# A graph kernel's relational sums in two steps: 128x32 masks for four chunks at a time, then seven quads per tile

## The chip, the cores and the metric

One core of one Trainium2 chip. The metric is the device time in microseconds (us), the median of three runs. Everything is float32. The profile comes from one execution of the same program.

## The reference, cut to what matters

The graph has 6250 nodes of 256 features and 106250 edges sorted by destination, one of them per node a self-loop; each edge has one of eight types. Three relational layers are followed by one attention layer:

```python
for l in range(3):
    xr = jnp.einsum('nd,rde->rne', x, W_rel[l])          # eight tables, one per edge type
    agg = jax.ops.segment_sum(xr[edge_type, src], dst, num_segments=N)
    x = jax.nn.relu(agg + x @ W_root[l] + bias[l])
# then h = x @ Wv + bv, scores q[src] + k[dst], softmax by dst, and the weighted sum of h[src]
```

A layer norm and a ReLU stand before the first layer and before the attention layer, and each of the two has a residual.

## The kernel before, in words

**Data.** Nodes are cut into 49 tiles of 128 (`NT`). A layer's eight transformed tables lie in DRAM, 1 MB per node tile. The edges without the self-loops are packed into 787 chunks of 128 (`CH`), in the order of their destination. Four chunks are a quad (called a group in the code), so there are 197 (`GROUPS`). Self-loops don't go through the chunks: VectorE adds them from PSUM when a table is made, and for the first layer from reloaded tables (`add_first_loops`, L814, eight multiply-adds per tile, whose running sum stands in PSUM).

**Gathers.** POOL runs `gather_pass` (L585) once per layer, four times in all: 787 indirect DMAs (L592), each fetching 128 rows of 1 KB into one slot of a ring of 40 (`RINGS` is 10 quads). Quad n may be issued when `released` has reached n - 9. That semaphore is counted by SP in `relay` (L716), a loop over the quads: it waits until quad n has landed, counts `in_order` (L721), then for quad m = n - 8 (`LAG`) it waits until every tile that reads quad m has gone far enough (`added`), and counts `released` (L732). SP's relay thus ties the release of one quad to the landing of the eighth after it. A pass can begin when all tables of the layer are stored (`wait_tables`).

**Relational sums.** Tile i reads 18 chunks (`SLOTS`) from a first chunk that is computed on the chip. ScalarE builds for each a 128x128 mask of edge against node (`build_mask`, L1344: 18 Abs, L1357, and five Relu, L1364). TensorE multiplies mask by ring slot 18 times into `sum_ps` (`sum_tile`, L1619, L1632), the 256-wide rows found through registers. A chunk is read by every tile that it touches. In the first layer the root product (L1625, two matmuls) opens the sum.

**The rest of a tile in the layers 0 and 1.** VectorE adds the loops' part and writes z (`sum_up`, L1042), TensorE transposes z (`turn`, L1531), ScalarE applies the ReLU (L1255), TensorE makes the next layer's table of the tile (`transform`, L1546: five banks, ten matmuls), ScalarE copies banks 0 to 2 to `stage` (L1264) and VectorE bank 3 (L785), VectorE adds the self-loops (L810) and the root part (L795), and ScalarE's queue stores 1 MB. The program order on TensorE puts the transform of tile i - 1 between the second and the third quad of tile i (L1656 to L1668). In layer 2 the transform is replaced by the product with Wv (`to_h`, L1678), after a layer norm on VectorE (L1067), and `store_h` writes 130 KB.

**Before the layers** the first table is made, 7.09 us per tile (the transform, L1546, back to back), and beside it DVE, POOL, ACT and PE plan the edges at fixed tiles (`before_layers_at`, L394). POOL ends its planning at L582. **The attention pass** (L1764 on) has its own chain of transposes, exponentials and sums (L1758), and the same `relay`.

The float32 matmul appears in the trace as two LDWEIGHTS records (PEld) and two MATMUL records (PE).

## Time and profile before

| what | value |
|---|---|
| median of three runs | 5282.95 us (5263.98 to 5283.96) |
| span of the profiled execution | 5218.2 us |
| time of the profiled execution outside its span | not recorded; the median stands 64.8 us above the span |
| PE / ACT / DVE / POOL busy | 3531.3 / 2203.5 / 1648.4 / 3049.7 us |
| before the layers | 0 to 369 us |
| layer 0 / layer 1 / layer 2, first gather to last | 369 to 1538 / 1588 to 2743 / 2786 to 3915 us |
| attention, first gather to last | 3950 to 5182 us |
| mean granted TensorE clock | 0.82 of 2.4 GHz |

Busy time counts an engine's own instructions. Register, branch and semaphore instructions aren't in it, so an engine can be "idle, issue" while its sequencer works on the next instruction. A releaser that reads "remote" or "issue" wasn't found by the profile.

### The profile page before, as it was taken

The page shows a single profiled execution, that of the slowest core. Times are in us where ns is not written, and L with a number is a line of the kernel's source. Part 1 is how long each engine was busy: PE and PEld are TensorE (multiplying, and loading weights), DVE is VectorE, ACT ScalarE, POOL GpSimd, SP SyncE. Part 2 cuts the span into 40 slices and gives each one's busy share as a digit, 9 for nine tenths or more (in the row PEclk, how much of TensorE's full clock was granted, in tenths as well). Part 3 has the DMA queues.
Part 4 walks back from the last instruction along what each step waited for, and adds up shares of the span by engine and source line. Part 5 has one row for each costly group of instructions (what it writes and reads, how often), then busy time and mean ns, then how long its engine had stood idle before and what let it go on. Part 6 is the DMA issues. An engine that isn't in the chain of part 4 may idle for free.

```text
span 5218.2 us, 55702 instructions
## 1 busy us (share of the span) xinstructions
PE 3531.3 (68%) x12674; PEld 2474.9 (47%) x12674; DVE 1648.4 (32%) x4423; ACT 2203.5 (42%) x6033; POOL 3049.7 (58%) x3295
## 2 busy tenths in 40 slices
PE   9986877788785777677775544545454666566666
PEld 4444554555553445445453333334333555455555
DVE  4533333334341222222221111111113444444444
ACT  2332443344432434343343333333334555555555
POOL 1135666666655666666664666666664566556664
PEclk9997988898887888888887777767677878878788
DMA  6554555555543444344443333333332333333332
GB/s 212 193 199 130 184 186 176 178 186 192 183 169 126 132 133 139 125 136 138 131 137 95 103 103 103 103 101 105 102 102 77 93 98 96 95 95 97 98 96 75
DMA packets 240046, 681.43 MB, mean 131 GB/s; under 512 B 60188, under 2 KB 111988, under 8 KB 215028
## 3 DMA queue, kind: packets, MB, share of 16 engines
q0 software_dynamic: 152400, 419.03, 27.6%
q10 hardware_dynamic: 57240, 186.43, 9.7%
q1 hardware_dynamic: 30092, 72.34, 3.8%
q8 instruction: 128, 2.10, 0.2%
q14 instruction: 186, 1.52, 0.1%
HBM read 501.99 MB, written 175.58 MB: 130 GB/s over the span
## 4 chain that ended last, share of the span: by engine, by line
PE 31%; another core or an unknown queue 28%; ACT 14%; issue 14%; DVE 9%; DVEq 2%; ACTq 1%; DMA 0%; SPq 0%; POOL 0%
PE bank L1546 13%; PE sum_ps L1632 9%; ACT masks L1357 4%; ACT masks L1451 4%; PE sum_ps L1758 3%; DVE root L810 3%; PE bank L1708 2%; DVEq L809 2%; ACT wide L1428 2%; PE bank L1714 2%; ACT masks L1364 1%; PE turn_ps L1531 1%; ACT stage L1467 1%; ACT wide L1461 1%
## 5 line engine op out<-in xcount | busy, mean ns | idle before, releaser
L592 POOL DMA_INDIRECT ring<-table,code x2361 | 2233.3, 946 | 1357.2 <-issue 661.9
L1632 PE MATMUL sum_ps<-ring,masks 128*128 x5292 | 1403.2, 423 | 199.2 <-issue 196.9
L1632 PEld LDWEIGHTS sum_ps<-ring,masks 128*128 128x128 f32 x5292 | 1126.6, 216 | 453.9 <-issue 271.2
L1546 PE MATMUL bank<-wide,xT 128*128 128x512 f32 (+1 forms) x2744 | 1125.2, 564 | 7.9 <-issue 6.3
L592 POOL DMA_INDIRECT ring<-h_table,code x787 | 746.6, 949 | 519.3 <-SPq L732 275.0
L1357 ACT ACTIVATE masks<-node_row,local 128x128 f32<-128x128 f32 x2646 | 788.5, 388 | 27.8 <-issue 13.7
L1546 PEld LDWEIGHTS bank<-wide,xT 128*128 128x128 f32 x2744 | 515.6, 190 | 563.6 <-issue 552.0
L1255 ACT ACTIVATE xT<-turn_ps 128x256 f32<-128x256 f32 x196 | 75.5, 385 | 1429.0 <-remote 587.4
L1758 PE MATMUL sum_ps<-ring,stage 128*128 x1764 | 492.7, 426 | 76.8 <-ACT stage L1467 48.7
L1264 ACT COPY stage<-bank 128x512 f32<-128x512 f32 x441 | 243.9, 582 | 590.0 <-remote 353.6
L810 DVE SCALAR_TENSOR_TENSOR root<-bank,loops,root 128x256 f32<-128x256 f32 x686 | 331.0, 483 | 369.5 <-ACT stage L1264 179.5
L1758 PEld LDWEIGHTS sum_ps<-ring,stage 128*128 128x128 f32 x1764 | 363.2, 218 | 143.4 <-issue 94.1
L1682 PE MATMUL bank<-wide,xT 128*128 128x256 f32 x196 | 94.5, 632 | 483.6 <-ACT xT L1255 475.0
L1714 PE MATMUL bank<-ident,wide 128*128 128x128 f32 x931 | 188.5, 337 | 333.0 <-ACT wide L1461 325.7
L1531 PE MATMUL turn_ps<-ident,z 128*128 128x128 f32 x392 | 99.7, 344 | 454.5 <-DVE z L1042 313.8
L1364 ACT ACTIVATE masks<-masks 128x512 f32<-128x512 f32 (+1 forms) x735 | 366.6, 573 | 85.6 <-remote 68.9
L1428 ACT ACTIVATE wide<-bank,low_key 128x512 f32<-128x512 f32 (+1 forms) x245 | 162.8, 665 | 502.5 <-remote 284.4
L810 DVE SCALAR_TENSOR_TENSOR root<-bank,loops,bias_row 128x256 f32<-128x256 f32 x98 | 47.4, 484 | 931.1 <-ACT stage L1264 560.2
L1070 DVE TENSOR_TENSOR stage<-sum_ps,root 128x256 f32<-128x256 f32 x49 | 20.8, 425 | 915.0 <-remote 834.5
L1714 PEld LDWEIGHTS bank<-ident,wide 128*128 128x128 f32 x931 | 142.2, 177 | 351.5 <-issue 351.2
L1531 PEld LDWEIGHTS turn_ps<-ident,z 128*128 128x128 f32 x392 | 53.3, 165 | 537.4 <-DVE z L1042 351.6
L1116 DVE SCALAR_TENSOR_TENSOR wide<-bank,key,wide 128x512 f32<-128x512 f32 (+1 forms) x245 | 177.1, 723 | 406.7 <-ACT wide L1428 309.0
(216 smaller groups left out, 2504.3 us busy)
## 6 DMA issues: line engine op xcount, KB each, us to landing
table<-stage ACTq DMA_DIRECT2D x96, 1024.0 KB
back<-table ACTq DMA_DIRECT2D x49, 1024.0 KB
table<-stage SPq DMA_DIRECT2D x48, 1024.0 KB
ring<-table,code POOLq DMA_INDIRECT x2361
ring<-h_table,code POOLq DMA_INDIRECT x787
h_table<-stage ACTq DMA_DIRECT2D x49, 130.0 KB
back<-h_table ACTq DMA_DIRECT2D x49, 130.0 KB
features<-xT SPq DMA_DIRECT2D x49, 128.0 KB, 4.0
```

The lines of the kernel that those rows point to most:

```text
L592: pool.indirect_dma_start(slot(c % RING, width), None, table, bass.IndirectOffsetOnAxis(ap=code[:, c:c + 1], axis=0)).then_inc(landed[n % ...
L810: nc.vector.scalar_tensor_tensor(root[:, i, :], bank[t // 2][:, t % 2 * D:(t % 2 + 1) * D], loop_weight(i, t), root[:, i, :] if t else bia ...
L1264: nc.scalar.copy(stage[:, b, 512 * q:512 * (q + 1)], bank[q][:, :]).then_inc(evacuated[q], 1)
L1357: instruction = nc.scalar.activation(masks[:, b, s, :], node_row[:, :], ACT.Abs, scale=-1.0, bias=local[:, bass.ds(i, 1), s])
L1364: instruction = nc.scalar.activation(part, part, ACT.Relu, scale=-1.0, bias=1.0)
L1428: return nc.scalar.activation(part, score_ps[c % 2][:, 0:part.shape[1]], ACT.Identity, scale=SLOPE, bias=low_key[:, bass.ds(i, 1)])
L1451: last = nc.scalar.activation(masks[:, b, s, :], node_row[:, :], ACT.Abs, scale=-1.0, bias=local[:, bass.ds(i, 1), s])
L1531: last = nc.tensor.transpose(turn_ps[:, k, :], z[:, b, k * P:(k + 1) * P], ident[:, :])
L1546: last = nc.tensor.matmul(bank[q][:, 0:width], xT[:, b, k, :], weights[:, k, 512 * q:512 * q + width], start=(k == 0), stop=(k == K - 1))
L1632: last = nc.tensor.matmul(sum_ps[b][:, 0:D], masks[:, b, s, :], at_offset(slots[s]), start=(s == 0 and l > 0), stop=(s == SLOTS - 1))
L1714: last = nc.tensor.transpose(attn_ps[c % 2][:, s % GROUP * P:(s % GROUP + 1) * P], scores[b][:, s * P:(s + 1) * P], ident[:, :])
L1758: last = nc.tensor.matmul(sum_ps[b][:, 0:D], attn_slot(s), at_offset(where[0][s]) if s < SLOTS else own_rows[:, b, 0:D], start=(s == 0), s ...
```

## The change

Chunk sums come first, tile sums second. For each quad, TensorE multiplies four 128x32 masks (edge against the chunk's own 32 nodes, counted from its least destination) by the four ring slots, each into 32 of the 128 PSUM partitions (`sum_windows`). ScalarE copies two quads' sums at a time to SBUF (`keep_pairs`). A tile is then the sum of seven quads, with seven 128x128 masks that name the node of each of the quad's 128 rows (`sum_tile`). Each chunk is read once, and quad n of the ring is issued when the chunk sums of quad n - 10 are done (`quad_done`), with no relay in between; SP's relay stays for the attention pass. VectorE builds both kinds of masks, two instructions per tile, and ScalarE builds none. On TensorE the transform of tile i - 1 stands in one piece behind the new pairs of quads of tile i and before its seven products. SP issues the loads and stores of the layers in place of ScalarE. The running sum of `add_first_loops` moves from PSUM to SBUF. Before the layers there are new planning steps for the masks: on DVE `relative`, `spread_quads` (nine small ones), `keep_relative` and `name_rows`, on PE seven transposes and one matmul, on POOL a few more of 343 elements. The attention pass is the same but for the names of its PSUM tiles. Most tiles bring two new pairs of quads (16 chunks).

```diff
-    PARTED = 1
+    WINDOW = P // GROUP
+    SPAN = 7
+    PAIR = 2
+    NP = -(-GROUPS // PAIR)
+    SUM_RING = 4
+    CHUNKS_AT_ONCE = 2 * PAIR * GROUP
+    MASK_BATCHES = -(-CH // CHUNKS_AT_ONCE)
...
+    def first_quad(t):
+        middle = CH * (P * t + P / 2) / N
+        return max(0, min(round((middle - GROUP * SPAN / 2) / GROUP), GROUPS - SPAN))
+
+    def pairs_to(t):
+        return (first_quad(t) + SPAN - 1) // PAIR + 1 if t >= 0 else 0
...
+    def new_pairs(t):
+        pairs = range(pairs_to(t - 1), pairs_to(t))
+        half = (len(pairs) + 1) // 2
+        return pairs[:half], pairs[half:]
...
-        sum_ps = [ctx.enter_context(nc.psum_tensor(f"sum_ps{b}", [P, 512], F32)) for b in range(2)]
-        turn_ps = ctx.enter_context(nc.psum_tensor("turn_ps", [P, K, P], F32))
+        pair_ps = [ctx.enter_context(nc.psum_tensor(f"pair_ps{b}", [P, 512], F32)) for b in range(2)]
+        both_sums = ctx.enter_context(nc.psum_tensor("both_sums", [P, 512], F32))
+        sum_ps = [both_sums[:, b * D:(b + 1) * D] for b in range(2)]
+        turn_root = ctx.enter_context(nc.psum_tensor("turn_root", [P, 512], F32))
...
+        def window_masks(k):
+            return flat(masks[:, k % 2, SPAN:SPAN + CHUNKS_AT_ONCE * WINDOW // P, :]
+                        ).rearrange("p (c w) -> p c w", w=WINDOW)
...
+        def quad_sums(q):
+            return pair_sums(q // PAIR)[:, q % PAIR * D:(q % PAIR + 1) * D]
...
+            step(pool.tensor_tensor(astray, per_chunk(chunk_id), per_tile(window_start), ALU.subtract))
+            step(pool.tensor_scalar(outside, astray, 0.0, None, ALU.is_lt))
+            step(pool.tensor_scalar(astray, astray, float(GROUP * SPAN - 1), None, ALU.is_gt))
+            step(pool.tensor_tensor(astray, astray, outside, ALU.add))
...
             def gather_pass(l, table, width):
                 if l:
-                    pool.wait_ge(in_order, l * GROUPS)
+                    pool.wait_ge(quad_done, l * GROUPS)
                 for n in range(GROUPS):
-                    if n >= RINGS:
-                        pool.wait_ge(released, l * RELEASES + n - RINGS + 1)
+                    if n >= RINGS and l < L:
+                        pool.wait_ge(quad_done, l * GROUPS + n - RINGS + 1)
+                    elif n >= RINGS:
+                        pool.wait_ge(released, n - RINGS + 1)
...
-            def relay(l):
+            def relay():
...
-                    sp.wait_ge(landed[n % RINGS], 16 * gathers_to(l, n))
+                    sp.wait_ge(landed[n % RINGS], 16 * gathers_to(L, n))
...
+            def load_features(i, b):
+                if i > 1:
+                    sp.wait_ge(added, tile_added(0, i - 2))
+                sp.dma_start(first_T[:, b, :, :].rearrange("p k n -> p (k n)"), features[i * P:(i + 1) * P, :]
+                             ).then_inc(features_loaded[b], 16)
+
+            def load_back(i, b):
+                if i > 1:
+                    sp.wait_ge(back_step, loops_done(i - 2, R))
+                sp.dma_start(back[:, b, :], tables_by_node[0][i * P:(i + 1) * P, :]).then_inc(back_loaded[b], 16)
+
...
+            def store_next(l, i, b):
+                for q in range(R // 2):
+                    sp.wait_ge(evacuated[q], CREDIT + NT * l + i + 1)
+                sp.dma_start(tables_by_node[l][i * P:(i + 1) * P, :], stage[:, b, :]).then_inc(stored[b], 16)
...
+                for i in range(NT):
+                    j, b = divmod(i, 2)
+                    if l == 0:
+                        load_features(i, b)
+                        load_back(i, b)
+                    if l == L - 1:
+                        load_x(i, b)
+                        if i > 1:
+                            store_h(i - 2, j - 1, b)
+                    elif i > 1:
+                        store_next(l + 1, i - 2, b)
...
-                    nc.vector.scalar_tensor_tensor(root[:, i, :] if t == R - 1 else loop_ps, back[:, b, t * D:(t + 1) * D],
-                                                   loop_weight(i, t), loop_ps if t else root[:, i, :], ALU.mult, ALU.add
-                                                   ).then_inc(back_step, 1)
-                settle(dve, loops_done(i, R))
+                    nc.vector.scalar_tensor_tensor(root[:, i, :], back[:, b, t * D:(t + 1) * D], loop_weight(i, t),
...
+            def mask_windows(l, first, end):
+                for k in range(first, end):
+                    chunks = range(CHUNKS_AT_ONCE * k, min(CHUNKS_AT_ONCE * (k + 1), CH))
+                    if l or k > 1:
+                        reused = l * GROUPS + (2 * PAIR * (k - 1) if k > 1 else 0)
+                        dve.wait_ge(quad_done, reused)
+                    shape = [P, len(chunks), WINDOW]
+                    nc.vector.tensor_tensor(window_masks(k)[:, 0:len(chunks), :],
+                                            rel_T[:, chunks[0]:chunks[-1] + 1].unsqueeze(2).to_broadcast(shape),
+                                            node_row[:, 0:WINDOW].unsqueeze(1).to_broadcast(shape), ALU.is_equal
+                                            ).then_inc(window_masked, 1)
+
+            def mask_tile(l, i):
+                if l or i > 1:
+                    dve.wait_ge(added, tile_added(l, i - 2) if i > 1 else tile_added(l - 1, NT - 1))
+                shape = [P, SPAN, P]
+                nc.vector.scalar_tensor_tensor(masks[:, i % 2, 0:SPAN, :],
+                                               row_node[:, first_quad(i):first_quad(i) + SPAN].unsqueeze(2).to_broadcast(shape),
+                                               -float(P * i), node_row[:, :].unsqueeze(1).to_broadcast(shape),
+                                               ALU.add, ALU.is_equal).then_inc(tile_masked, 1)
+
+            def upcoming_masks(l, i):
+                if i < NT:
+                    mask_tile(l, i)
+                    mask_windows(l, batches_to(i - 1), batches_to(i))
+
...
+            def relative():
...
+                shape = [P, KM, P]
+                nc.vector.tensor_tensor(rel_n.rearrange("p (m e) -> p m e", e=P), dst_n.rearrange("p (m e) -> p m e", e=P),
+                                        least.unsqueeze(2).to_broadcast(shape), ALU.subtract).then_inc(row_step, 1)
...
+            def name_rows():
+                dve.wait_ge(row_step, ROWS_PLACED)
+                dve.wait_ge(shift_known, 1)
+                nc.vector.tensor_scalar(row_node[:, :], pair_ps[0][:, 0:KM * WINDOW], row_place[:, 0:1], far_shift[:, 0:1],
+                                        ALU.add, ALU.add).then_inc(row_step, 1)
...
+                for i in range(NT):
                     j, b = divmod(i, 2)
...
+                    sum_up(l, i, j, b)
+                    upcoming_masks(l, i + 2)
+                    if l == 0 and i + 1 < NT:
+                        add_first_loops(i + 1, (i + 1) // 2, 1 - b)
+                    next_table(l, i, j, b)
...
-            def build_mask(l, i, j, b, last=False):
...
-                for s in range(SLOTS):
-                    instruction = nc.scalar.activation(masks[:, b, s, :], node_row[:, :], ACT.Abs, scale=-1.0,
-                                                       bias=local[:, bass.ds(i, 1), s])
...
-                for c in range(PIECES):
-                    part = masks[:, b, gathered(c)[0]:gathered(c)[-1] + 1, :]
-                    instruction = nc.scalar.activation(part, part, ACT.Relu, scale=-1.0, bias=1.0)
-                instruction.then_inc(mask_ready[b], 1)
...
+            def keep_pairs(l, pairs):
+                for p in pairs:
+                    act.wait_ge(quad_done, l * GROUPS + min(PAIR * (p + 1), GROUPS))
+                    if l or p >= SUM_RING:
+                        act.wait_ge(added, tile_added(l, tiles_of_pair(p - SUM_RING) - 1) if p >= SUM_RING
+                                    else tile_added(l, -1))
+                    width = D * (min(PAIR * (p + 1), GROUPS) - PAIR * p)
+                    nc.scalar.copy(pair_sums(p)[:, 0:width], pair_ps[p % 2][:, 0:width]).then_inc(pair_kept, 1)
...
+                for i in range(NT + 1):
+                    early, late = new_pairs(i) if i < NT else ((), ())
+                    keep_pairs(l, early)
+                    if i:
+                        j, b = divmod(i - 1, 2)
+                        use = (l + 1) * USES[b] + j
+                        relu_turned(use, b, transformed[b], NB * use)
+                    keep_pairs(l, late)
+                    if i:
+                        for q in range(R // 2 - 1):
+                            keep_bank(l + 1, use, b, q)
...
+            def turn_relative():
+                pe.wait_ge(row_step, ROWS_SPREAD)
+                pe.wait_ge(broken_copied, 1)
+                turn_edges(rel_n, row_step)
...
+            def sum_windows(l, pairs):
+                for p in pairs:
+                    if l or p > 1:
+                        pe.wait_ge(pair_kept, l * NP + p - 1 if p > 1 else l * NP)
+                    for q in range(PAIR * p, min(PAIR * (p + 1), GROUPS)):
+                        k = GROUP * q // CHUNKS_AT_ONCE
+                        pe.wait_ge(window_masked, l * MASK_BATCHES + k + 1)
+                        pe.wait_ge(landed[q % RINGS], 16 * gathers_to(l, q))
+                        for c in chunks_of(q):
+                            at_row = c % GROUP * WINDOW
+                            last = nc.tensor.matmul(pair_ps[p % 2][at_row:at_row + WINDOW, q % PAIR * D:(q % PAIR + 1) * D],
+                                                    window_masks(k)[:, c % CHUNKS_AT_ONCE, :], slot(c % RING, D),
+                                                    start=True, stop=True)
+                        last.then_inc(quad_done, 1)
+
+            def sum_tile(l, i, j, b):
+                pe.wait_ge(tile_masked, l * NT + i + 1)
+                pe.wait_ge(pair_kept, l * NP + pairs_to(i))
+                if l == 0:
+                    pe.wait_ge(features_loaded[b], 16 * (j + 1))
                     for k in range(K):
                         nc.tensor.matmul(sum_ps[b][:, 0:D], first_T[:, b, k, :], first_root[:, k, :],
                                          start=(k == 0), stop=False)
-                for c in pieces:
-                    settle(pe, l * GROUPS + groups[c])
-                    pe.wait_ge(mask_ready[b], use + 1)
-                    pe.wait_ge(in_order, l * GROUPS + groups[c])
-                    for s in gathered(c):
-                        last = nc.tensor.matmul(sum_ps[b][:, 0:D], masks[:, b, s, :], at_offset(slots[s]),
-                                                start=(s == 0 and l > 0), stop=(s == SLOTS - 1))
-                    if c in PART_ENDS:
-                        last.then_inc(added, 1)
...
+                for i in range(NT + 1):
+                    early, late = new_pairs(i) if i < NT else ((), ())
+                    sum_windows(l, early)
+                    if i:
+                        j, b = divmod(i - 1, 2)
+                        turn_sum(l, j, b)
+                    sum_windows(l, late)
+                    if i:
+                        transform((l + 1) * NT + i - 1, (l + 1) * USES[b] + j, b, AHEAD + REST)
+                    if i < NT:
+                        sum_tile(l, i, i // 2, i % 2)
```

## Rows read from the trace of the kernel before

**Rows 1.** The page's first line: the span.
```profile
span 5218.2 us, 55702 instructions
```
**Rows 2.** Busy time by stretch, all engines; the columns are in its first line.
```profile
core 0: us, PE busy (x) PEld busy (x) DVE busy (x) ACT busy (x) POOL busy (x), PEclk, DMA share, GB/s
...
369.00:1538.00 1169.00, 900.69 (x3007) 617.17 (x3008) 444.35 (x998) 467.95 (x1292) 743.65 (x786) 0.86 0.54 181
...
1588.00:2743.00 1155.00, 829.10 (x2713) 552.95 (x2714) 239.34 (x507) 463.85 (x1287) 742.84 (x786) 0.84 0.42 134
...
2786.00:3915.00 1129.00, 562.40 (x1968) 427.27 (x1968) 166.04 (x640) 408.68 (x1197) 743.46 (x786) 0.71 0.35 103
```
**Rows 3.** Groups of instructions, the gathers: busy us, mean ns | idle before them.
```profile
L592 POOL DMA_INDIRECT ring<-table,code x2361 | 2233.3, 946 | 1357.2 <-issue 661.9 <-SPq L732 560.0 <-DMA table<-stage 135.4
...
L592 POOL DMA_INDIRECT ring<-h_table,code x787 | 746.6, 949 | 519.3 <-SPq L732 275.0 <-issue 244.3
```
**Rows 4.** Timeline of POOL: first and last gather of each pass (start us, us).
```profile
369.55 1.11 POOL L592 DMA_INDIRECT ring<-table,code  x1 [43.42 <-DMA table<-stage]
...
1538.44 0.95 POOL L592 DMA_INDIRECT ring<-table,code  x1 [0.30 <-issue]
1588.72 0.94 POOL L592 DMA_INDIRECT ring<-table,code  x1 [49.34 <-DMA table<-stage]
...
2743.29 0.94 POOL L592 DMA_INDIRECT ring<-table,code  x1 [0.30 <-issue]
2786.85 0.94 POOL L592 DMA_INDIRECT ring<-table,code  x1 [42.62 <-DMA table<-stage]
...
3915.69 0.95 POOL L592 DMA_INDIRECT ring<-table,code  x1 [0.30 <-issue]
3950.09 0.94 POOL L592 DMA_INDIRECT ring<-h_table,code  x1 [33.46 <-issue]
```
**Rows 5.** Timeline of one tile's wait in layer 2, POOL and DVE.
```profile
3026.65 0.95 POOL L592 DMA_INDIRECT ring<-table,code  x1 [0.30 <-issue]
3027.90 0.95 POOL L592 DMA_INDIRECT ring<-table,code  x1 [0.30 <-issue]
...
3031.94 0.94 POOL L592 DMA_INDIRECT ring<-table,code  x1 [3.10 <-SPq L732]
...
3032.21 0.42 DVE L1074 SCALAR_TENSOR_TENSOR root<-stage 128x256 f32<-128x256 f32 x1
...
3033.19 0.95 POOL L592 DMA_INDIRECT ring<-table,code  x1 [0.30 <-issue]
```
**Rows 6.** Timeline of DVE: the first masked chunk of the attention pass.
```profile
3956.84 0.95 DVE L1181 TENSOR_SCALAR masks<-masks,ring 128x128 f32<-128x128 f32 x4 [10.51 <-issue]
```
**Rows 7.** Timeline of PE: root product in layer 0, then the end of layer 1.
```profile
1554.78 1.03 PE L1625 MATMUL sum_ps<-first_root,first_T 128*128 128x256 f32 x4
...
2769.47 4.48 PE L1632 MATMUL sum_ps<-ring,masks 128*128 x20
2774.53 0.44 PE L1531 MATMUL turn_ps<-ident,z 128*128 128x128 f32 x2 [0.57 <-DVE z L1042]
2775.44 8.00 PE L1546 MATMUL bank<-wide,xT 128*128 128x512 f32 x20 [0.47 <-ACT xT L1255]
```
**Rows 8.** Groups of instructions: weight loads, masks, copies, first loops and a wide VectorE operation.
```profile
L1632 PEld LDWEIGHTS sum_ps<-ring,masks 128*128 128x128 f32 x5292 | 1126.6, 216 | 453.9 <-issue 271.2
...
L1357 ACT ACTIVATE masks<-node_row,local 128x128 f32<-128x128 f32 x2646 | 788.5, 388 | 27.8 <-issue 13.7 <-DMA table<-stage 9.2 <-DVE stage L785 2.4
...
L1264 ACT COPY stage<-bank 128x512 f32<-128x512 f32 x441 | 243.9, 582 | 590.0 <-remote 353.6 <-PE bank L1546 188.2 <-issue 47.6
...
L821 DVE SCALAR_TENSOR_TENSOR bank<-back,loops,bank 128x256 f32<-128x256 f32 x294 | 143.4, 488 | 32.8 <-issue 2.3 <-DVE bank L821 0.5
...
L944 DVE SCALAR_TENSOR_TENSOR masks<-ring,masks 128x896 f32<-128x896 f32 x1 | 1.1, 1093 | 0.0
```
**Rows 9.** Timeline of POOL: the end of its planning.
```profile
326.05 0.09 POOL L582 MEMSET credit<- 1x1 f32 x1 [1.85 <-DMA need<-need_dram]
```

346 lines of the change are left out of this document (158 added, 188 removed).

## The prediction, made before the changed kernel was seen

> **What bounds the kernel now.** I read the profile in four steps. First the busy times by stretch [rows 2]: in the three layers TensorE is busy for 77, 72 and 50% of the time, ScalarE 40, 40 and 36%, DMA 54, 42 and 35%. None is full. POOL has the same 743 us in all three, and that looks low too, but busy time leaves out its issue work. So second, the gathers in a row [rows 5]: they start 1.25 us apart (3026.65, 3027.90; 3031.94, 3033.19) though each lasts 0.95. The missing 0.30 us is "issue", and it makes most of the 661.9 us behind "issue" in the group's row [rows 3]. A pass of 787 gathers can't be shorter than 786 x 1.25 = 982.5 us. Third, what a pass takes from its first gather to its last [rows 4]: 1168.9 in layer 0, 1154.6 in layer 1, 1128.8 in layer 2. So POOL is the bound for 85% of each layer, and the rest is waits: 186.4 + 172.1 + 146.3 = 504.8 us. The group's row names them: 560.0 us behind SP's L732, the relay's "released" [rows 3] (some 0.3 us in each is issue time that is there anyway).
>
> Fourth, why it waits [rows 5]: the gather at 3027.90 ends at 3028.85, the next starts 3.1 us later, in a layer in which TensorE is half idle. The ring isn't full of unread work; the release of a quad is tied to the landing of the eighth after it, so that POOL is let go only two quads ahead of what has landed, and to a tile's second part. A landing takes about 2.0 us: the fourth gather of the attention pass ends at 3950.09 + 3 x 1.25 + 0.95 = 3954.8 [rows 4], and the first mask that reads its quad starts at 3956.84 [rows 6]. That latency is paid again and again.
>
> **The change, part by part.** My yardstick is 787 / 49 = 16.06 gathers per tile, 20.1 us.
>
> *The release.* Quad n now waits only for the chunk sums of quad n - 10. Those come one or two quads at a time, and in between TensorE does one transform and one tile's sum, 8.0 us and 3.1 us. POOL has ten quads, 50 us, in the ring, so it should never wait as long as TensorE needs less than 20.1 us per tile. All 504.8 us then go. This is nearly the whole forecast, so the next step is the one that matters.
>
> *TensorE per tile.* A 256-wide record costs 4.48 / 20 = 0.224 us, hence 0.448 us per mask product, and a transform 8.0 us, a transpose pair 0.44 [rows 7]. Before: 18 x 0.448 + 8.0 + 0.44 = 16.5 us in layer 1 (busy 829 / 49 = 16.9 [rows 2] agrees). After: 7 x 0.448 = 3.1, plus 8.0, plus 0.44, plus 16 chunk products. No row has a product with 32 columns. Its nearest row has 128 columns and the same 256-wide moving side: 0.448, as if the four column groups went one after the other; a quarter of it, 0.112, if they went side by side. I keep both ends: 7.2 or 1.8 us. Layer 1 is then 18.7 or 13.3 us, layer 0 with its root product (1.03 [rows 7]) 19.8 or 14.3, layer 2 with a product by Wv of the same size as that 11.8 or 6.4. I take the nearest row, 0.448. All lie below 20.1, in layer 0 by only 0.3. TensorE's work may thus rise and the layers still get shorter. The clock weighs against this: it was granted at 0.84 in layer 1, that is, 32% of the time at 1.2 GHz, with the engine 28% idle. With 13.3 us of work at that mean clock the engine needs 15.8 us and stays inside; with 18.7 us it is nearly never idle and I expect the clock up, but at 0.93 it would be at 20.1.
> The Trainium skill (TensorEngine Tiling (Array Packing), "Key Properties") says that different tiles load weights and multiply in parallel, but that a change of the tiling mode drains the engine, which this change does four times a tile. No row here shows either. By the first, the work would be near 13 to 15 us and the sum the same.
>
> *ScalarE.* It loses the masks, 18 x 0.388 us (788.5 in all) and the Relus behind them, and gets two copies of pairs per tile at 0.58 [rows 8]. Neither ended a wait above: nothing gained but slack, and 1.2 us of new copies that lie under the transform. They cost nothing while the transform covers them; without it 1.2 us a tile.
>
> *VectorE.* It gets a mask of 896 elements, 1.09 us by the only operation of that size, and one of 512, some 0.65 by the same row's scale [rows 8]. With the table's ten operations (some 6 us) and, in layer 0, eight first loops at 0.49 (3.9 us) it has about 12 us of 20.1. The window masks wait for chunk sums that come behind the transpose on TensorE, so VectorE holds back the loops and the table's evacuation until the transform starts, and ends them some 10 us later, before the tile's sum (12 us). Cost 0; cover 2 us in layer 0.
>
> *SP.* Loads and stores of a layer move behind waits on one in-order queue: a store of tile i - 2 stands before the loads for tile i + 1. Each is wanted a whole tile (20 us) later; cost 0. In the relay's place nothing waits on SP in the layers.
>
> *POOL's pace beside VectorE.* The new masks read two SBUF operands, and so do the first loops now. The nearest row: L1074, with two SBUF operands, lies wholly inside the gather of 3031.94, which took 0.94 us and was followed after 0.30 [rows 5]. I take 3 us per pass for odd delays, +9 us (0 to 20).
>
> *Between two passes.* E is the end of the last gather. Quad 195 has landed at E - 1.75; its chunk sums are done near E. Then in order: transform 46 (8.0), sum of tile 47 (3.1), three chunks (1.3), transpose (from it to the transform's start 0.91 [rows 7]), transform 47 (8.0), sum of tile 48 (3.1), 0.6 for VectorE's z, 0.91 and, from the last transform's start to the next pass, 2786.85 - 2775.44 = 11.4 [rows 4, 7]. Sum 37.3, and 1.0 more in layer 0, against 42.6 and 49.3: -5.3 and -11.0. In layer 2 the last tile has 11 products fewer behind the last landing, 11 x 0.448: -5. Together -21 (0 to -35).
>
> *Before the layers.* DVE gets one subtraction of 896 elements (1.09 [rows 8]) and some fifteen smaller ones, PE seven transposes. TensorE sets the pace there, and DVE has 4 to 5 us free per tile, so part is hidden: +8 (0 to +16, all of them at 1.09). POOL's extra planning (some 5 us) ends against a slack of 369.55 - 326.05 = 43.5 us [rows 4, 9]: 0. The attention pass isn't touched: 0.
>
> **The sum.** -504.8 + 9 - 21 + 8 = -509 us. On the profiled execution 5218.2 [rows 1] - 509 = 4709. Its own time around the span isn't recorded; the median stands 64.8 us above it and I carry that over: 5282.95 - 509 = **4774 us**.
>
> **Rivals.**
> 1. *TensorE becomes the bound in the layers 0 and 1.* The chunk products cost 0.448, and drains or stretches at 1.2 GHz take another tenth: 18.7 / 0.9 = 20.8 and 19.8 / 0.9 = 22.0 us per tile, (0.7 + 1.9) x 49 = 127 us: **4901** (4820 to 5000). For it: the margin of 0.3 us, and the transform in one piece, which bunches the work. Against: products with a quarter of the columns should take less than the full ones.
> 2. *VectorE's masks hold up POOL.* Each new microsecond with two SBUF operands delays the gathers by as much: (8 x 0.42 + 1.7) us per tile in layer 0, 1.7 in each other layer, (5.1 + 1.7 + 1.7) x 49 = 417 us: **5191**. Against it stands the gather around L1074 [rows 5]. The Trainium skill (SBUF — State Buffer, "SBUF: two separate sides") has this as its rule: the two engines share a port pair, and a VectorE instruction with two SBUF inputs locks out a GpSimd one that reads SBUF. The trace's gather of 0.94 us doesn't show it.
> 3. *Slower: the small products can't hide their weight loads.* Place: between a quad's eight record pairs. A load takes 0.216 us [rows 8] and lies beside the matmuls today. Laid bare it adds 0.43 us per chunk, 6.9 us per tile: 25.6 us in layer 1, 26.7 in layer 0, (5.5 + 6.6) x 49 = 593 us: **5367**. It decides from the point at which the two excesses eat 509 us, that is 10.4 us in all: (10.4 + 1.7) / 32 = 0.38 us bare per chunk. Against it: a load of 32 columns should be shorter than one of 128, and loads overlap in every burst of the trace. The Trainium skill (TensorE: Matmul & The Clock Gate, "Part 3: Packing small matmuls") says that a load passes matmuls in flight only when its row group differs, which it doesn't among these four. For full-size products the trace disagrees: 20 records at 0.224 us each [rows 7], with loads of 0.216 beside them.
> 4. *The waits stay*, because something else than the relay holds the ring, such as the first chunk sums being late at each pass. The change would bring the tails and cost the planning, 5283 - 21 + 8 = **5270**. Against: 10 quads are 50 us.
>
> **How the numbers follow.** Forecast 0.70; rival 1 0.19; rival 2 0.04; rival 3 0.05; rival 4 0.02, within 0.5% of before (about what a measurement of this kernel can tell from no change). The range takes the forecast's own bounds (down to 4746: no delays, nothing added ahead, longer tails saved) and rival 1 to its end at 5000; left out are the rivals 2 to 4, 0.11, and a few per cent of bad luck. Faster 0.93, same 0.02, slower 0.05.
>
> **What would show it.** Right: the first gather to the last takes 983 to 990 us in each of the three layers, starts stay 1.25 us apart, and POOL's waits for a semaphore inside a pass nearly vanish; TensorE idles for landings; the gap between passes is 35 to 40 us. The length of a quad's burst (8 records x 0.224 = 1.8 us, or a quarter) tells which price the products have. Wrong: passes 0 and 1 well over 990 us with TensorE always busy (rival 1, or 3 if the burst exceeds 3 us), gathers longer than 1 us beside masks (rival 2), or POOL waiting on `quad_done` while TensorE idles (rival 4). The forecast fails as a whole if layer 2, which has 8 us to spare, isn't near 985.

## The result: half a per cent, not ten

The changed kernel takes **5249.31 us** (median of 7, 5236.56 to 5251.97) against 5281.34 us (7 runs, 5263.16 to 5283.96) for the one before in the same job (a job is one set of runs on one chip): ratio **0.9946**, 95% interval 0.9932 to 0.9959. Two later jobs gave 0.9956 (0.9942 to 0.9970) and 0.9953 (0.9929 to 0.9977). In one more job, of which more below, both kernels took 13 to 16% less and the order turned round: 4542.19 us (4 runs, 4538.37 to 4545.96) against 4436.48 us (7 runs, 4433.76 to 4440.49), ratio **1.0238**, interval 1.0221 to 1.0256. Every run here, timed or not, was recorded by the profiler.

The work per engine fell as the change says. The page's first lines for the changed kernel:

```profile
span 5249.8 us, 48781 instructions
## 1 busy us (share of the span) xinstructions
PE 3232.7 (62%) x14171; PEld 1974.0 (38%) x14171; DVE 1905.0 (36%) x4736; ACT 1240.1 (24%) x2949; POOL 3146.9 (60%) x3305
```

ScalarE lost 963 us, TensorE 299 us, and VectorE, which builds the masks now, gained 257 us. But the passes are as long as they were. Busy time by stretch, the four passes in order, answering [rows 2] (each stretch runs from the pass's first gather to its last):

```profile
core 0: us, PE busy (x) PEld busy (x) DVE busy (x) ACT busy (x) POOL busy (x), PEclk, DMA share, GB/s
375.90:1542.40 1166.50, 777.98 (x3418) 430.21 (x3419) 513.44 (x1066) 150.23 (x274) 775.63 (x786) 0.80 0.54 178
1599.30:2739.30 1140.00, 718.59 (x3130) 372.20 (x3131) 313.58 (x588) 150.94 (x274) 762.54 (x786) 0.77 0.42 134
2793.50:3925.90 1132.40, 451.94 (x2434) 275.59 (x2434) 238.69 (x717) 82.47 (x184) 779.67 (x787) 0.63 0.36 102
3965.10:5211.00 1245.90, 773.40 (x3591) 637.63 (x3591) 571.25 (x1676) 698.80 (x1859) 749.07 (x786) 0.78 0.35 95
```

Passes of 1166.5, 1140.0 and 1132.4 us stand against 1168.9, 1154.6 and 1128.8 [rows 4], and POOL's time above 1.25 us per gather is 184, 158 and 150 us against 186, 172 and 146: 491 us in the layers where the prediction had 504.8 going to nothing. The gathers' groups, answering [rows 3]:

```profile
L674 POOL DMA_INDIRECT ring<-table,code x2361 | 2320.8, 983 | 1273.7 <-issue 733.1 <-remote 378.7 <-DMA table<-stage 96.7
L674 POOL DMA_INDIRECT ring<-h_table,code x787 | 750.0, 953 | 535.1 <-SPq L814 285.8 <-issue 249.3
```

SP has gone from the layers' row. In its place stands "remote", a releaser that the profile didn't find. It is `quad_done`, the only semaphore POOL still waits for there. One tile of layer 1, in the timelines of POOL, DVE and PE:

```profile
2008.22 0.95 POOL L674 DMA_INDIRECT ring<-table,code  x1 [0.30 <-issue]
...
2013.23 0.95 POOL L674 DMA_INDIRECT ring<-table,code  x1 [0.30 <-issue]
2017.38 0.95 POOL L674 DMA_INDIRECT ring<-table,code  x1 [3.20 <-remote]
...
2006.05 0.42 DVE L924 TENSOR_TENSOR root<-turn_root,root 128x256 f32<-128x256 f32 x1
2017.05 0.42 DVE L1233 TENSOR_TENSOR z<-both_sums,root 128x256 f32<-128x256 f32 x1 [10.58 <-remote]
...
2004.91 3.19 PE L1767 MATMUL both_sums<-masks 128*128 128x256 f32 x14
2008.02 1.07 PE L1753 MATMUL pair_ps<-ring,masks 128*32 128x256 f32 x16
2017.53 0.69 PE L1644 MATMUL turn_root<-ident,z 128*128 128x128 f32 x2 [8.44 <-DVE z L1233]
```

By its records TensorE ends the tile's sum at 2008.1 and two pairs of windows at 2009.1. VectorE's z, which needs nothing but that sum, starts at 2017.05, 9 us later, 2.9 us after POOL's last gather ended. In the semaphores' own records `added` goes up at 2017.03 and `quad_done`, twice, at 2017.12 and 2017.21, though the two records that count it start at 2008.28 and 2008.71. So POOL waits for a signal from TensorE, and here gets it only once POOL itself has stopped. The other tiles agree: the middle value of z's delay behind its sum is 7.4 us in layer 0 and 8.1 us in layer 1. In layer 2 only 17 of 46 are over 2 us, but POOL's 32 waits there end 8.9 us (middle value) behind the last record of the chunk sums. That is the same picture as one tile before the change [rows 5], where I had read the relay into it.

### The profile page after: what moved, and what is told of

It reads as the page before. It is cut to its first block, busy times and chain, and to the rows that moved or that the text cites. A ratio compares the mean times of both kernels' runs of the same rounds, so it can differ in the third digit from the quotient of the medians.

```text
span 5249.8 us, 48781 instructions
## 1 busy us (share of the span) xinstructions
PE 3232.7 (62%) x14171; PEld 1974.0 (38%) x14171; DVE 1905.0 (36%) x4736; ACT 1240.1 (24%) x2949; POOL 3146.9 (60%) x3305
## 4 chain that ended last, share of the span: by engine, by line
PE 36%; another core or an unknown queue 34%; issue 13%; ACT 9%; DVE 7%; DVEq 0%; ACTq 0%; POOL 0%; DMA 0%; POOLq 0%
PE bank L1659 19%; PE pair_ps L1753 5%; PE pair_ps L1864 3%; PE both_sums L1767 3%; ACT masks L1565 3%; ACT wide L1542 2%; DVE root L939 2%; PE turn_root L1644 2%; PE bank L1814 2%; PE bank L1820 1%; ACT stage L1581 1%; ACT wide L1575 1%; DVE z L1233 1%; PE bank L1796 1%
## 5 line engine op out<-in xcount | busy, mean ns | idle before, releaser
L674 POOL DMA_INDIRECT ring<-table,code x2361 | 2320.8, 983 | 1273.7 <-issue 733.1
L1659 PE MATMUL bank<-wide,xT 128*128 128x512 f32 x2352 | 1148.9, 644 | 45.0 <-ACT xT L1445 44.7
L674 POOL DMA_INDIRECT ring<-h_table,code x787 | 750.0, 953 | 535.1 <-SPq L814 285.8
L1767 PE MATMUL both_sums<-masks 128*128 128x256 f32 x2058 | 539.7, 420 | 340.5 <-ACT masks L1501 206.3
L1501 ACT COPY masks<-pair_ps 128x512 f32<-128x512 f32 x297 | 173.2, 583 | 2184.5 <-remote 1693.8
L1767 PEld LDWEIGHTS both_sums<-masks 128*128 128x128 f32 x2058 | 441.0, 216 | 431.8 <-issue 358.2
L1864 PE MATMUL pair_ps<-ring,stage 128*128 x1764 | 508.4, 437 | 136.4 <-issue 91.3
L1753 PE MATMUL pair_ps<-ring,masks 128*32 128x256 f32 x4722 | 442.8, 491 | 99.7 <-DMA ring<-table,code 76.2
L1864 PEld LDWEIGHTS pair_ps<-ring,stage 128*128 128x128 f32 x1764 | 371.1, 223 | 205.3 <-issue 154.2
L939 DVE SCALAR_TENSOR_TENSOR root<-bank,loops,root 128x256 f32<-128x256 f32 x686 | 331.1, 483 | 161.3 <-ACT stage L1507 73.2
L1565 ACT ACTIVATE masks<-node_row,local 128x128 f32<-128x128 f32 x931 | 282.1, 396 | 0.0
L1371 DVE TENSOR_SCALAR masks<-masks,ring 128x128 f32<-128x128 f32 x882 | 203.0, 298 | 213.7 <-issue 212.7
L1753 PEld LDWEIGHTS pair_ps<-ring,masks 128*32 128x32 f32 x4722 | 148.9, 129 | 295.4 <-issue 242.4
```

The costliest lines, as they stand in the source:

```text
L674: pool.indirect_dma_start(slot(c % RING, width), None, table, bass.IndirectOffsetOnAxis(ap=code[:, c:c + 1], axis=0)).then_inc(landed[n % ...
L939: nc.vector.scalar_tensor_tensor(root[:, i, :], bank[t // 2][:, t % 2 * D:(t % 2 + 1) * D], loop_weight(i, t), root[:, i, :] if t else bia ...
L1371: last = nc.vector.tensor_scalar(masks[:, b, s, :], masks[:, b, s, :], -FAR, source, ALU.mult, ALU.add)
L1565: last = nc.scalar.activation(masks[:, b, s, :], node_row[:, :], ACT.Abs, scale=-1.0, bias=local[:, bass.ds(i, 1), s])
L1659: last = nc.tensor.matmul(bank[q][:, 0:width], xT[:, b, k, :], weights[:, k, 512 * q:512 * q + width], start=(k == 0), stop=(k == K - 1))
L1753: last = nc.tensor.matmul(pair_ps[p % 2][at_row:at_row + WINDOW, q % PAIR * D:(q % PAIR + 1) * D], window_masks(k)[:, c % CHUNKS_AT_ONCE, ...
```

## The experiments

Two words for what follows: a record is one of the two MATMUL entries that a product leaves in the trace, and a pause is a stretch in which POOL issues no gather. The theories I took in turn: A, TensorE's last signals come out only when more products follow; B (B1), gathers without a pause hold TensorE up; B2, the rows' data do; B3, a budget of instructions; C, the records are early and TensorE has more work than they show; L, a fixed price per pause; R, a rate.

**e1: more products.** 24 products of 128x256 before a tile's turn in layers 0 and 1.

```
+    ...                                       # waits until bank[0] is free
+    for _ in range(24):
+        nc.tensor.matmul(bank[0][:, 0:D], ident[:, :], weights[:, 0, 0:D], start=True, stop=True)
     turn_sum(l, j, b)
```

> 24 extra products of 128x256 into an idle bank stand on TensorE between a tile's early windows and its turn in layers 0 and 1 (about 2.6 us per tile, in an idle stretch of some 8 us). The changed kernel's trace shows TensorE's signal of a tile's sum 6.5 to 9 us after the sum's last product, about 2.7 us after GpSimd's last gather of a run. Theory A (TensorE's last signals come out only when more products follow): VectorE's z starts within 1 us of the sum's end, GpSimd's waits in layers 0 and 1 (340 us) mostly go, time 4900 to 5000 us. Theory B (the signals are held up while GpSimd issues gathers back to back, whatever TensorE does): z still 6 to 9 us late, waits and time unchanged, 5235 to 5265 us. Theory C (the products' records are early, and TensorE really computes until the signal comes): the extra products come on top, about 2.6 us per tile, 5249 + 98 x 2.6 = 5500 us.

5466.64 us. I had counted a product as one record of 0.11 us; it is two of 0.22, so the edit added 10.6 us per tile and made TensorE the bound: tiles of 24.8 and 24.3 us in layers 0 and 1, TensorE busy throughout. z mostly came 0.04 to 0.9 us after its sum, but with POOL stopped. Nothing was told apart. (5466.64 us lies near what theory C had, but by the added 10.6 us per tile, not by C's reason.)

**e2: a quarter of the gathers** in layers 1 and 2.

```
-    for c in chunks_of(n):
+    for c in (chunks_of(n) if l in (0, L) else chunks_of(n)[:1]):
```

> In layers 1 and 2 only one chunk in four is gathered (the other slots of the ring keep old rows), so GpSimd has 5 us of gathers per tile in place of 20. It shows what the other four engines need by themselves. If the tile's own chain of products, copies and masks takes 23 us, as long as the pass of now (theory C): layers 1 and 2 stay at 1130 to 1140 us each. If the signals are held up by back-to-back gathers (theory B): GpSimd is quiet nearly always, z follows the sum within 0.5 us, and the two passes fall to what the engines need, 13 to 19 us per tile, 640 to 930 us each. Theory A (more products must follow): z stays 2 to 9 us late in the quiet kernel too, passes over 950 us.

4064.2 us. POOL's timeline in layer 1:

```profile
1749.62 1.40 POOL L674 DMA_INDIRECT ring<-table,code  x1 [8.16 <-PE pair_ps L1753]
1751.32 0.94 POOL L674 DMA_INDIRECT ring<-table,code  x1 [0.30 <-PE pair_ps L1753]
...
1762.93 1.41 POOL L674 DMA_INDIRECT ring<-table,code  x1 [8.16 <-PE pair_ps L1753]
```

A tile takes 13.31 us, z follows its sum by 0.04 us, the passes take 616 and 462 us. Layer 0 of the same run, with all its gathers, has z 7.45 us behind its sum (middle value of 45 tiles). The chain of a tile is short when POOL is quiet: C falls as a matter of work, and so does A.

**e3: by itself.** TensorE and VectorE signal back and forth, with and without gathers.

> A kernel of its own that computes nothing of the reference: TensorE does two products of 128x256 and signals, VectorE copies the sum out and signals back, in rounds; in phases without gathers, beside 80 gathers of GpSimd without a pause (100 us), the same with 24, with 4 further products and with 16 small ones (128x32) behind each signal, with ScalarE in TensorE's place, and beside 48 plain loads of SP. Theory B: beside gathers a round with TensorE takes many us (the signals come out only as the gathers stop), with ScalarE and beside plain loads 1 to 1.5 us. Theory A: rounds beside gathers are long with nothing behind the signal and short with 24 products behind it. Theory C, or anything that belongs to the kernel and not to the chip: every round takes 1 to 1.6 us (3.5 to 4 us with 24 products behind), with or without gathers.

Windows of the run, the first without gathers, the next two in the first phase with them, then the one with 24 further products and the one with ScalarE asking:

```profile
core 0: us, PE busy (x) PEld busy (x) DVE busy (x) ACT busy (x) POOL busy (x), PEclk, DMA share, GB/s
5.00:30.00 25.00, 20.16 (x40) 11.23 (x38) 3.97 (x10) 0.00 (x0) 0.00 (x0) 1.00 0.00 0
35.00:58.00 23.00, 18.36 (x37) 10.55 (x36) 3.81 (x9) 0.00 (x0) 17.52 (x19) 1.00 0.36 108
66.00:122.00 56.00, 10.37 (x20) 5.88 (x20) 2.12 (x5) 0.00 (x0) 42.39 (x45) 1.00 0.35 105
225.00:280.00 55.00, 11.72 (x20) 5.94 (x21) 0.42 (x1) 0.00 (x0) 41.59 (x45) 0.51 0.35 105
555.00:582.00 27.00, 4.53 (x21) 3.64 (x20) 11.72 (x33) 13.13 (x33) 20.60 (x22) 0.66 0.35 106
```

Nine rounds beside the gathers take 2.59 us as in quiet. Then TensorE does 20 product records in 56 us, **2.80 us each**, at a granted clock of 1.00 as at 0.51, until 8 to 12 us behind the last gather. With ScalarE in its place a round takes 0.76 to 0.98 us beside the same gathers; beside 48 plain loads of SP (235 GB/s) TensorE's take 1.65 us, and the same behind the loads (shorter than the 2.59 us of the first phase, for which I have no reason). B holds, and the kernel isn't needed for it.

**e4: what about the gathers does it.**

> A kernel of its own again: rounds of two products of 128x256, a signal and 24 further products (52 product records, 11.2 us without gathers), beside 80 gathers. In the ping-pong run before, TensorE did some 40 to 50 product records at full speed beside back-to-back gathers and then one per 2.80 us until some 10 us after the last gather. Eight phases, each with one thing changed: as it was; the 24 products with 64 columns; gathered rows of 64 columns (256 bytes); a small memset of GpSimd behind each gather (about 0.3 us); a wait for landing after every 8 gathers; bf16 operands in the 24 products; a wait for landing after every 4 gathers; 240 memsets in place of the gathers. Theory B1 (GpSimd's unbroken issuing of gathers blocks TensorE's instructions, whatever they read): 2.8 us per record also with 64 columns, with narrow rows and with bf16; the memsets alone do nothing; a wait after every 8 gathers brings TensorE back to 11.2 to 14 us per round. Theory B2 (the rows' data in SBUF are in the way of what TensorE reads): with 64 columns or with narrow rows the cost per record falls to a quarter, 0.7 us, or goes. Theory B3 (a budget of instructions that only long quiet gives back): the waits after 8 or 4 gathers change nothing, rounds stay over 50 us.

One window from each of the first seven phases, in the order of the text above:

```profile
core 0: us, PE busy (x) PEld busy (x) DVE busy (x) POOL busy (x), PEclk, DMA share, GB/s
20.00:100.00 80.00, 21.01 (x46) 11.02 (x44) 0.42 (x1) 60.51 (x65) 0.54 0.35 105
220.00:300.00 80.00, 9.44 (x31) 8.54 (x30) 0.00 (x0) 53.77 (x57) 0.50 0.32 95
445.00:525.00 80.00, 17.91 (x30) 8.73 (x31) 0.42 (x1) 58.41 (x62) 0.50 0.12 26
635.00:715.00 80.00, 80.00 (x372) 70.42 (x372) 2.97 (x7) 64.98 (x103) 1.00 0.28 84
755.00:835.00 80.00, 80.00 (x373) 70.42 (x372) 2.97 (x7) 47.44 (x51) 1.00 0.28 83
890.00:960.00 70.00, 9.46 (x28) 3.63 (x28) 0.00 (x0) 52.94 (x57) 0.52 0.35 105
1010.00:1090.00 80.00, 80.00 (x372) 70.44 (x371) 2.97 (x7) 40.83 (x44) 1.00 0.24 72
```

After the fast start (which is in the first window), some 30 records in 80 us whether they have 256 or 64 columns, float32 or bf16 operands, and whether the gathers move 105 or 26 GB/s: B2 falls. With 0.30 us more between gathers, or a wait for landing after 8 or 4, TensorE does 372: B1 holds, B3 falls. In the eighth phase, 240 memsets in place of the gathers, it does 520 in 116 us, at full speed too.

**e5, e6, e7: room between the gathers.** GpSimd writes a spare tile behind each quad (128x256) or each gather (128x1); e7 does the like by itself.

```
+    def space():
+        pool.wait_ge(prep_step, steps[0])
+        steps[0] += 1
+        pool.memset(spare[:, :], 0.0).then_inc(prep_step, 1)
...
+    if (c + 1) % 4 == 0:
+        space()
```

> The changed kernel with one memset of 128x256 (0.30 us) by GpSimd behind each quad of gathers, in all four passes: 0.08 us more per gather, 1.2 us per tile of 16 gathers. Theory B1 (unbroken issuing of gathers at 1.25 us starves TensorE's instructions, 2.80 us each, and the ring then fills): the pause per quad is enough, or nearly, TensorE's signals come within 1 us, GpSimd's waits of 3 us per tile go, a pass of the layers takes about 197 x (5.0 + 0.3) = 1045 us in place of 1132 to 1166, and the time is 4900 to 4980 us (below that if the attention's pass gains too). Rival (GpSimd waits for TensorE because the tile's chain of products, copies and masks takes 23 us whatever the gathers do): the memsets only fill waits, passes stay at 1130 to 1170 us, time 5240 to 5260 us. Rival (a pause per quad is too seldom): waits stay and 236 us come on top, up to 5485 us.

> The same with a memset of 128x1 (about 0.06 us and its own start) behind each single gather. Theory B1 with the distance between two gathers as what counts: a step of 1.31 to 1.45 us per gather, passes of 1030 to 1140 us without any wait, time 4850 to 5250 us by that step. If the short memset hides in the gather's own gap (the step stays at 1.25 us) and any other instruction between two gathers is enough to let TensorE go on, passes come down to 985 us and the time to 4750 us. Rival (the chain takes 23 us per tile): unchanged, 5240 to 5260 us.

> The ping-pong kernel with 80 gathers per phase and rounds of 52 product records (11.2 us alone). GpSimd's memset between gathers: 128x1 behind each, 128x256 behind every 4th, 128x1 behind every 4th, 128x64 behind every 4th, 128x256 behind every 8th, 128x64 behind every 2nd, and no memset but a wait that is already met behind each. In the run before, 0.30 us behind each gather gave 11.2 us in every round, nothing between them 2.80 us per product record. Theory B1 (what counts is how dense the gathers are): there is a mean step between 1.25 and 1.55 us from which the rounds are clean; the 0.30 us behind every 4th (1.33 us mean) are near it, the short ones behind every 4th and the wait alone stay bad. Rival (what counts is that GpSimd executes another instruction at all): all of them are clean, the wait alone perhaps too.

4666.23 and 4540.18 us, passes of 1050 to 1024 and 1014 to 998 us, and the passes look like a hit for B1 until one sees the kernel before beside them: **4431.09 us**. In e7 nothing was slow, not even with no memset at all. So this job was in another condition, and the three runs say nothing on spacing, but much on the condition. What differs is written in the trace: of the 3148 x 16 = 50,368 updates that the gathers' landings make, the traces of e5 and e6 hold 50,179 and 50,048, those of before and after 11,263 and 12,723. I call the two kinds "free" (over 99% of the updates kept, TensorE not held up) and "held" below. In the three free traces with the kernel z follows its sum by 0.04 us in the middle, beside gathers mostly 1.25 us apart.

**e8, e9, e10: once more.** The job was of the held kind again, on the same chip number as the free one.

> The changed kernel once more, in three rounds, because the kernel before took 5212 and 5274 us on the chips of four of the runs so far and 4431 us on the chip of the last three, where the trace keeps all 16 landing updates of a gather (50,400 in the run) and the ping-pong rounds are 11.2 us with nothing between the gathers; in the traces of before and after only some 11,300 and 12,700 of them are kept. Theory B1 with the chip as its condition (some chips starve TensorE beside unbroken gathers, some do not): on a chip where before takes 5210 to 5280 us, this takes 5237 to 5252 us; on one where before takes about 4431 us it takes about the same, 4400 to 4450 us, because GpSimd's steps of 1.25 us bound both. Rival (the change is worth something or costs something by itself once nothing is held up): over 1% from before on such a chip.

> The changed kernel with the memset of 128x1 behind each gather, again in three rounds beside before and the changed kernel on one chip. On a chip of the quick kind it repeats 4540 us, 2.5% over before (waits behind each gather cost 0.02 us and more). On a chip of the kind where before takes 5210 to 5280 us: theory B1 says the little room is enough to keep TensorE's signals prompt, 4540 to 4700 us, 10% or more under both kernels; if it is not enough, 5250 to 5300 us.

> The seven spacings again. On a quick chip: 11.2 us in every round, 793 us. On a chip of the other kind the phases differ: clean with 0.30 us behind every 4th gather, not clean with a met wait alone (2.8 us per product record, rounds of 50 to 100 us) by theory B1; all clean if any instruction between two gathers is enough.

e8 5197.65 us; e9 5213.86 us, 0.9983 (0.9971 to 0.9995) of before, so the memset of 128x1 brings nothing where it was to bring 10%. In e10 all seven spacings are slow, 0.30 us behind every fourth gather too. Windows of the first two phases and the last, then GpSimd in the first phase:

```profile
35.00:100.00 65.00, 29.77 (x43) 12.06 (x42) 0.00 (x0) 47.84 (x91) 0.50 0.31 92
220.00:290.00 70.00, 16.16 (x28) 7.60 (x27) 0.42 (x1) 55.52 (x69) 0.50 0.34 101
...
1210.00:1280.00 70.00, 14.86 (x26) 7.47 (x26) 0.00 (x0) 52.95 (x57) 0.50 0.35 105
```

```profile
67.51 0.10 POOL L83 MEMSET spare<- 128x1 f32 x1 [0.84 <-remote]
67.75 0.94 POOL L74 DMA_INDIRECT ring<-in_x_dram,code  x1
```

The phases are not equally slow, and TensorE is not the only one held up. With a memset behind each gather (the first phase) TensorE does a record in 1.43 us, with one of 128x64 behind every second in 2.20 us, in the others in 2.64 to 2.84 us (from 40 us into a phase on). In the first, GpSimd itself waits ten times for 0.8 us or more for the signal of its own last memset, which is in no way TensorE's, and its gathers stand 1.42 us apart in place of 1.25 in e7; with 128x64 behind every second they stand 1.43 us apart in place of 1.27 (from the 36th gather on).

**e11, e12: fewer and more instructions of TensorE.**

```
-    for s in range(SPAN):                     # e11, and k in range(1) in the transform
+    for s in (0, 1, SPAN - 1):
...
+    for _ in range(8):                        # e12, before the turn; its two waits left out
+        nc.tensor.matmul(bank[0][:, 0:16], ident[:, :], weights[:, 0, 0:16], start=True, stop=True)
```

> The changed kernel with less on TensorE per tile: three of the seven products of a tile's sum, and one of the two halves (k = 0) in each of the transform's products behind the layers' sums; the rest of both is left out. Per tile of layers 0 and 1 that is 50 product records in place of 68 and some 8 us of TensorE in place of 14. On a chip where before takes 5.2 to 5.3 ms: theory B1 with the number of TensorE's instructions as what counts (some 45 to 50 records pass freely between two pauses of GpSimd, further ones take 2.8 us each) says the last few records of a tile are no longer late: GpSimd's waits of 145 to 165 us in a pass of layers 0 and 1 fall below 60, time 4950 to 5100 us. Rival (every signal of TensorE at the end of a burst waits for a pause, however few records there are): GpSimd still waits once per tile, time 5150 to 5240 us. On a chip of the quick kind: about 4430 us, and nothing told apart.

> The changed kernel with 8 further products of 128x16 columns per tile into an idle bank between the early windows and the turn, in layers 0 and 1: 16 more product records, 84 in place of 68, but only some 1 us of TensorE's time in an idle stretch of 8 us. On a chip where before takes 5.2 to 5.3 ms: with the number of instructions as what counts, they come on top at up to 2.8 us each until GpSimd pauses a second time per tile: 0.5 to 3 us more per tile, time 5240 to 5500 us. Rival (TensorE's time or the chain counts): they lie in idle time, time unchanged within 15 us of the changed kernel's. On a chip of the quick kind about 4430 us.

5151.99 and 5218.10 us (before 5217.13). With 50, 68 (e8, another held job) and 84 records per tile, layer 1 takes 1121.0, 1127.2 and 1133.0 us: 12 us between the ends. Of the 66 us between e11 and e12, 39 lie in the three gaps between the passes. Inside a pass, how much TensorE has to do, in work or in instructions, is nearly without effect; the rival stood, and the count of instructions that B1 was given with it fell.

**e13 to e16: the pauses themselves.**

```
+    if n % 2 == 0 and n and l < L:            # e14
+        pool.wait_ge(landed[(n - 1) % RINGS], 16 * gathers_to(l, n - 1))
...
-    pool.wait_ge(quad_done, l * GROUPS + n - RINGS + 1)
+    if (n - RINGS) % 8 == 0:                  # e15
+        pool.wait_ge(quad_done, l * GROUPS + min(n - RINGS + 8, GROUPS - RINGS))
```

> The changed kernel beside the one before again, for the two conditions seen: where before takes 5.2 to 5.3 ms this takes 0.4 to 0.6% less; if before takes about 4431 us here (one set of runs so far), this takes 4400 to 4450 us, since GpSimd's steps of 1.25 us bound both, and only the tails between the passes differ.

> The changed kernel, with GpSimd waiting in layers 0 to 2 after every 8 gathers until the last of them has landed. In the ping-pong kernel this kept TensorE at full speed. So far every kernel's pass is 983 us plus one pause of 2.6 to 3.2 us per unit of credit (49 per pass in the layers, 98 in the attention), whatever TensorE has to do. Theory L (a pause costs what the last landing and the signals behind it take, some 2.0 to 3.0 us, and frees TensorE; what counts is how many there are): 98 pauses in place of 49, passes of 983 + 98 x (2.0 to 2.6) = 1180 to 1240 us, TensorE's signals prompt, time 5350 to 5550 us. Rival (the waits have to do with TensorE's chain of a tile and lie in parallel to pauses): the forced pauses take the place of the others, passes stay at 1120 to 1150 us, time 5190 to 5260 us.

> The changed kernel, with GpSimd taking its credit in layers 0 to 2 for eight quads (two tiles) at once: it pauses every 32 gathers, until all but two quads of the ring are consumed, in place of every 16. Theory L with the number of pauses alone: 25 pauses of 3 us, passes of 1060 us, time 4960 us. Theory L with TensorE starved in between: TensorE gets through about one tile beside the gathers and has to do the second in the pause, 13 us, so passes of 983 + 25 x (13 + 3) = 1380 us, time 5900 us. Between them the runs show how much of TensorE's work goes on beside the gathers.

> The changed kernel with a memset of 128x256 behind every second gather, a mean step of 1.40 us, in all passes. In the ping-pong kernel 1.55 us kept TensorE quick and 1.33 us (behind every fourth) did not. If 1.40 us are enough, the pauses go and a pass takes 787 x 1.40 = 1102 us in the layers and in the attention: 120 to 130 us less in the attention, 20 to 40 in each layer, time 5000 to 5070 us, under both kernels. If they are not, waits of 2.6 us per unit come on top of part of it: passes of 1140 to 1240 us, time 5200 to 5350 us. In the other condition 787 x 4 x 0.15 = 470 us over before, 4900 us.

e13: 5196.07 us. e14: 5464.19 us, passes of 1267, 1223 and 1225 us. POOL's timeline, 8 gathers and a wait of 2.5 us, 12.2 us in all; z follows its sum by 0.04 us in every layer:

```profile
2002.93 0.94 POOL L676 DMA_INDIRECT ring<-table,code  x1 [2.53 <-DMA ring<-table,code]
...
2015.12 0.94 POOL L676 DMA_INDIRECT ring<-table,code  x1 [2.47 <-DMA ring<-table,code]
```

e15: 5836.66 us, POOL and PE over 61 us of layer 1:

```profile
2387.07 0.98 POOL L675 DMA_INDIRECT ring<-table,code  x1 [20.84 <-PE pair_ps L1754]
...
2425.94 0.95 POOL L675 DMA_INDIRECT ring<-table,code  x1 [0.30 <-issue]
2448.06 0.97 POOL L675 DMA_INDIRECT ring<-table,code  x1 [21.17 <-PE pair_ps L1754]
...
2410.14 0.69 PE L1645 MATMUL turn_root<-ident,z 128*128 128x128 f32 x2 [8.68 <-issue]
...
2433.03 9.84 PE L1660 MATMUL bank<-wide,xT 128*128 128x512 f32 x16 [16.50 <-ACT xT L1446]
```

32 gathers at full speed, in which TensorE gets through about one tile, and then 21 us of POOL waiting while it does the other. e14's time lies inside what was written for it (theory L), only its first pass is 27 us longer. e15's passes are 1463, 1415 and 1143 us: the first two near the 1380 us written for a starved TensorE, the third not, and 5836.66 us in all comes near the 5900 partly by luck. e16: 5192.44 us, 0.9928 (0.9890 to 0.9965) of before but no better than e13 in the same job; 1572 memsets of 0.33 us took the place of waits, and the passes stayed 1139.6, 1132.0, 1122.0 and 1237.1 us.

**e17, e18.**

> The ping-pong kernel (80 gathers per phase, rounds of 52 product records, 11.2 us alone) with a memset of 128x64, 128x128, 128x192 behind each gather, 128x256 behind every second and behind each, and nothing. Theory R (what the chip can pass on of gathers and TensorE together has a rate; a pass of the kernel in the slower condition comes to 1120 to 1150 us for 787 gathers, 1.42 to 1.46 us per gather, with no memsets, with short ones behind each and with long ones behind every second): below about 1.42 us per gather TensorE is held up sooner or later, the later the nearer, above it never. So long rounds with 64 columns, with 128 if its step is below 1.4 us, at most a few late ones with 256 behind every second (1.40 us), none with 192 (about 1.47 us) and 256 behind each (1.55 us). Rival (a certain idle time of GpSimd is needed each time, 0.3 us at least): long rounds with 192 columns too.

> The changed kernel beside the one before a fourth time. In the slower condition 0.4 to 0.6% less than before (5190 to 5250 us against 5220 to 5280 us). In the quick condition, if it is met, 4400 to 4450 us against about 4431 us: no difference beyond 0.5%, with GpSimd at 1.25 us per gather through every pass.

This job was of the free kind. e17 was clean in every phase, with nothing between the gathers too, so the rate wasn't found. e18 gave the 4542.19 against 4436.48 us above, where 4400 to 4450 had been expected. Its gathers' groups and the four passes:

```profile
L674 POOL DMA_INDIRECT ring<-table,code x2361 | 2312.2, 979 | 838.3 <-issue 746.9 <-DMA table<-stage 80.7 <-PE pair_ps L1753 10.7
L674 POOL DMA_INDIRECT ring<-h_table,code x787 | 750.6, 954 | 273.2 <-issue 256.5 <-SPq L814 16.7
```

```profile
377.10:1392.10 1015.00, 777.96 (x3528) 429.02 (x3532) 531.13 (x1098) 151.29 (x282) 775.41 (x786) 0.86 0.63 209
1431.80:2436.70 1004.90, 718.37 (x3240) 371.05 (x3240) 320.94 (x604) 151.28 (x282) 765.27 (x787) 0.82 0.48 154
2474.00:3482.30 1008.30, 468.56 (x2504) 262.61 (x2504) 248.20 (x747) 86.88 (x191) 768.67 (x786) 0.66 0.40 115
3507.70:4506.00 998.30, 750.17 (x3599) 629.46 (x3600) 559.65 (x1685) 690.88 (x1864) 749.55 (x787) 0.83 0.43 118
```

The waits for semaphores are gone, in the attention too, whose relay the change didn't touch: 16.7 us behind SP where the same kernel waits 285.8 in a held job. What is left above 1.25 us is in the gathers themselves. POOL and DVE in layer 1:

```profile
2070.60 0.94 POOL L674 DMA_INDIRECT ring<-table,code  x1 [0.30 <-issue]
2071.85 1.41 POOL L674 DMA_INDIRECT ring<-table,code  x1 [0.30 <-issue]
2073.56 0.95 POOL L674 DMA_INDIRECT ring<-table,code  x1 [0.30 <-issue]
...
2070.76 1.08 DVE L969 SCALAR_TENSOR_TENSOR masks<-row_node,node_row 128x896 f32<-128x896 f32 x1
2071.75 0.68 DVE L960 TENSOR_TENSOR masks<-rel_T,node_row 128x512 f32<-128x512 f32 x1
```

The gather of 2071.85 starts 0.10 us into the window masks and takes 0.46 us longer than its neighbours. The one of 2070.60 has the wider tile masks beside it and takes 0.94: it had started first. In layer 1, 46 of 787 gathers take over 1.05 us, all beside L960 or L969, 19.9 us together; in layer 0, 105, nearly all beside these and the first loops (L949), 29.7 us; in layer 2, 89, 23.2 us, 35 of them beside L1282, an operation with two SBUF operands that stood there before too. All of them started inside a VectorE operation; of the 146 gathers that had started before one of these four did, none took over 1.05 us. In the trace of before, of a held job, there are 9 such gathers in the three layers.

A PSUM operand makes the difference for the first loops. Before, with their running sum in PSUM, 74 gathers started inside one that reads it there (L821) and none took over 1.05 us; in the changed kernel's first trace, with the sum in SBUF (L949), 89 of 137 did.

## Why the prediction was wrong, step by step

**The release: the step that failed.** This is the term of 504.8 us, of which 13 came. I wrote that POOL "is let go only two quads ahead of what has landed", and that with ten quads in the ring "all 504.8 us then go". The waits didn't come from the relay. It is SP that POOL waited for, but SP passed on `added`, TensorE's signal; in e18 the same relay with the same distance costs 16.7 us. What sets the waits in a held job is that TensorE's signals are held up: beside unbroken gathers it soon does one product record in 2.80 us (e3), it falls behind while POOL runs (e15), the ring fills, POOL stops, and that stop lets TensorE catch up. A direct wait on `quad_done` meets the same stop. Where nothing is held up (e18) `quad_done` ends 10.7 us of POOL's waits in the layers and the relay 16.7 us in the attention. What is not shown is how the 2.80 us of e3 come about inside the kernel, whose records have their usual lengths and only their signals are late, and whose passes hardly feel 34 records more or fewer per tile (e11, e12). My evidence was a row that named a releaser and a wait with an idle TensorE in it; I didn't ask when TensorE's last signal had come. The trace of before had it. Its timeline around [rows 5], the last sum before POOL's gap on PE, and the operation on DVE that needs nothing but that sum:

```profile
3015.70 4.48 PE L1632 MATMUL sum_ps<-ring,masks 128*128 x20
...
3031.75 0.42 DVE L1070 TENSOR_TENSOR stage<-sum_ps,root 128x256 f32<-128x256 f32 x1 [18.55 <-remote]
```

The products end at 3020.18 by their records and VectorE starts 11.6 us later, 0.2 us before POOL's next gather. These rows could be read then, and they speak against the term.

**Rival 4** ("the waits stay ... 5270") is what happened, at a chance of 0.02. Its reason, something other than the relay, was right; its argument against, "10 quads are 50 us", is the same mistake.

**TensorE per tile.** The lower bound was right: 16 records in 1.07 us are 0.13 us per chunk product against 0.112 and 0.448, so four column groups do run side by side. e2's tile of 13.31 us is the low sum of 13.3. Having taken the nearest row, 0.448, cost nothing here, since neither sum decided; that is luck. Rivals 1 and 3 fall with it; bare weight loads of 32 columns would show in those 1.07 us.

**ScalarE, VectorE, SP.** Nothing in the passes shows a price for ScalarE or for VectorE's cover, as said (ScalarE's masks came to 788.5 / 147 = 5.4 us per tile, not 18 x 0.388 = 7.0, as they overlap; nothing hung on it); no row names SP in the layers any more. VectorE's price lay elsewhere:

**POOL's pace beside VectorE: +9 us forecast, +79 to +88 found** (2312.2 and 2320.8 us for 2361 gathers against 2233.3 [rows 3]). The nearest row was a bad one: L1074 starts at 3032.21, inside a gather that began at 3031.94 [rows 5], and the delay only strikes a gather that starts inside the VectorE operation. The Trainium skill (SBUF — State Buffer, "SBUF: two separate sides") says that whichever starts first gets the shared ports for the whole instruction and the other waits. e18's two gathers agree; the other direction doesn't show, as L969 takes 1.08 us in the middle in the 126 cases in which it starts inside a gather as in the 21 in which it doesn't. Rival 2 priced each microsecond of mask and first loop in full, 417 us; about a sixth of it came true, 67 us beside L949, L960 and L969 in e18. In held jobs it lies beside POOL's waits, and how much of it they take in isn't known. In the free job it is most of the loss: +7.5 us before the first gather (377.1 against 369.6), some 79 us here, and about 20 us left for the gaps and tails, against 105.7 us between the medians. There is no trace of the kernel before from such a job, so the last split is an estimate.

**Between passes: -21 forecast.** In the held job of the result the gaps grew, 56.9, 54.2 and 39.2 us against 50.3, 43.6 and 34.4. In the free one they are 39.7, 37.4 and 25.4, near the 38.3 and 37.3 I had summed; the sum fits only where nothing is held up (its links weren't measured one by one).

**Before the layers: +8** forecast, +6.3 found (375.9 against 369.6).

**The range.** Its lower end, 4746, is a slip of 3 us: 5282.95 - 504.8 - 35 is 4743. It decides nothing, as the time lies above the upper end of 5000, where only the rivals 2 to 4 had been.

**The half per cent.** e8's job stands at the profiled execution's level, so its trace can be set against it: passes of 1145.6, 1127.2, 1120.1 and 1233.9 us, -23, -27, -9 and +2 us; gaps +28, start +6, end +1; -22 us in all (5195.9 against 5218.2). The passes gain 57 us, the gaps give half of it back. What in the shorter work gained it wasn't separated; the two traces are also of different jobs.

## What to carry to other kernels

A wait's named releaser is only the last link: before costing its removal, follow the signal back to the instruction that gave it and compare the two times. If they are many microseconds apart, the wait belongs to whatever holds the signal, and a shorter path from it doesn't remove the wait. Put VectorE operations with two SBUF operands where no gather starts, or give one operand in PSUM (in e18, none of the 271 gathers that started inside L939 with its PSUM operand took over 1.05 us, and 81 of the 91 inside L969 did), and compare two kernels in more than one job when their bound is a stream of gathers from GpSimd.

## What the runs showed of the hardware that I had not expected

- TensorE beside gathers that GpSimd issues every 1.25 us without a pause, in a held job: full speed for 9 to 27 us after a rest, then about 2.80 us per product record, of 256 as of 64 columns, until some 5 to 20 us after the last gather (e3, e4, e10). ScalarE and VectorE, signalling to each other, aren't slowed (0.76 to 0.98 us a round in e3); GpSimd's signals to itself come late (e10). A pause of 2.5 us after 8 gathers, or 0.30 us after each (1.55 us per gather), avoids it in e4; 0.30 us after every fourth doesn't (e10).
- It comes with lost records: 11,252 to 16,709 of 50,368 landing updates in the held traces with all gathers (25,805 with e14's pauses), over 50,000 in the free ones. Inside one run the two go together as well: the phases of e4 in which TensorE is slow keep 14 to 16% of their updates, the three with gathers in which it is not keep 75, 49 and 66%. So records are lost even where TensorE keeps its speed. Of the seven jobs with experiments two were free, on chip numbers 4 and 14, and one of the held ones was on 4 too, so it isn't the chip alone. The Trainium skill (NOTIFIC — the notification-queue block, "7.1 Overflow: three behaviours, one of which stalls the engine") says that an overfull record path either drops records or holds its producer back. Lost updates would follow from the first and a slow TensorE from the second, if different records meet different ends. It was not tested, as no run here went unrecorded, and another cause shared by both isn't excluded.
- Also open is whether a held pass is set by the pauses it needs or by a rate. e8, e9, e11, e12, e13 and e16 all take 1118 to 1152 us per pass of the layers, 1.42 to 1.46 us per gather, with nothing, short or long memsets between the gathers and 50 to 84 records per tile. e14 and e15 fit pauses; e10, whose GpSimd falls to 1.42 and 1.43 us per gather with no tile's chain to wait for, speaks for a rate, though TensorE is slow there all the same; e17, which was to find the rate, met a free job. The 0.30 us behind each gather that e4 found enough was not tried in the kernel in a held job.
- No version tried beats both kernels in both conditions: the change is 0.5% ahead when held and 2.4% behind when free.
